# A graph network with mixtures of experts: layer 2's choice of experts moved into the mixture's own stage

## What is computed

```python
h = relu(x @ sW1 + sb1); h = relu(h @ sW2 + sb2); shared = h @ sW3 + sb3     # 256 -> 256 -> 128 -> 256
all_out = the same with 4 experts, 256 -> 128 -> 64 -> 256, for every node
gates = softmax(x @ gW + gb)               # 4 values for each node
topv, topi = top_k(gates, 2)
topw = softmax(topv)                       # of the two chosen gate values
out = shared + sum over the two chosen of topw * all_out[expert]
```

## Time and profile before

| | us |
|---|---|
| median of 3 runs | 3898.34 (3896.64 to 3900.64) |
| the profiled execution, its own time | 3903.26 |
| its span, from the first to the last instruction | 3901.5 |
| TensorE busy | 3152.4 (81%) |
| VectorE busy | 1736.2 (45%) |
| ScalarE busy | 1019.9 (26%) |
| GpSimd busy | 2350.9 (60%) |

### The profile page before, as it was taken

One profiled execution on the slowest core, in us unless ns is written; L12 is line 12 of the kernel. 1 busy time (PEld: TensorE's weight loads), 2 busy tenths in 40 slices (PEclk: granted clock), 3 DMA queues, 4 the chain that ended last, 5 costly groups with the idle time before them and its releaser, 6 DMA issues.

```text
span 3901.5 us, 49195 instructions
## 1 busy us (share of the span) xinstructions
PE 3152.4 (81%) x16263; PEld 2193.2 (56%) x16264; DVE 1736.2 (45%) x4543; ACT 1019.9 (26%) x2155; POOL 2350.9 (60%) x1900
## 2 busy tenths in 40 slices
PE   4999965377787885898079999988998798786798
PEld 3555554256456655788068888875454333334565
DVE  5555545735576775100721112233444444443344
ACT  3666632213546541233221100012120000001121
POOL 6888888888676776677666665540000777772221
PEclk9999996678899995999589999998999655765899
DMA  8663231122557545778444443320213533337232
GB/s 295 183 183 58 5 40 1 1 19 2 163 127 197 135 104 123 209 206 209 80 111 144 137 139 128 133 67 32 95 64 105 150 105 104 103 105 177 74 126 72
DMA packets 284516, 440.11 MB, mean 113 GB/s; under 512 B 167039, under 2 KB 213523, under 8 KB 270565
## 3 DMA queue, kind: packets, MB, share of 16 engines
q1 hardware_dynamic: 118978, 285.09, 23.4%
q0 software_dynamic: 164448, 147.39, 19.4%
q10 hardware_dynamic: 864, 4.80, 0.3%
HBM read 318.97 MB, written 117.63 MB: 112 GB/s over the span
## 4 chain that ended last, share of the span: by engine, by line
PE 38%; POOL 32%; issue 10%; DVE 10%; DMA 7%; DVEq 1%; SPq 1%; ACT 1%; POOLq 0%; ACTq 0%; PEldq 0%
POOL count_cells L484 16%; PE g_acc L2220 14%; POOL g3g_got L1241 9%; PE f2m_pR L2901 4%; POOL weight_cells L1193 4%; PE f3e_pH L3231 3%; PE f2m_pR L2873 3%; PE f3e_pY L3240 3%; DMA f1e_xs<-table,f_node 2%; PE g_acc L1772 2%; DMA g3g_got<-relations,g3g_idx 2%; PE f2m_pO L2884 1%; DMA count_cells<-cells_count,added_row 1%; DMA weight_cells<-added_weight,added_row 1%; PE g_psL L2203 1%
## 5 line engine op out<-in xcount | busy, mean ns | idle before, releaser
L1193 POOL DMA_INDIRECT weight_cells<-added_weight,added_row x391 | 630.5, 1612 | 235.7 <-issue 118.2
L484 POOL DMA_INDIRECT count_cells<-cells_count,added_row x391 | 655.2, 1676 | 141.2 <-issue 118.3
L1241 POOL DMA_INDIRECT g3g_got<-relations,g3g_idx x416 | 398.5, 958 | 545.2 <-ACTq L101 418.8
L2220 PE MATMUL g_acc<-g_H,g_blocks 125*125 125x256 f32 x2500 | 557.3, 382 | 25.6 <-DMA g_blocks<-weight_cells 25.0
L2220 PEld LDWEIGHTS g_acc<-g_H,g_blocks 125*125 125x125 f32 x2500 | 468.6, 189 | 95.6 <-issue 25.4
L2131 POOL DMA_INDIRECT slots_dram<-sort_rec,sort_row x392 | 378.1, 964 | 237.6 <-issue 115.1
L1254 PE MATMUL g3g_pp<-g3g_got,g3g_hot 128*125 128x256 f32 x832 | 436.7, 642 | 104.6 <-DMA g3g_got<-relations,g3g_idx 91.2
L1254 PEld LDWEIGHTS g3g_pp<-g3g_got,g3g_hot 128*125 128x125 f32 x832 | 192.9, 283 | 348.5 <-DMA g3g_got<-relations,g3g_idx 343.4
L1030 ACT ACTIVATE X<-same_scores 128x128 bf16<-128x128 f32 (+7 forms) x392 | 254.7, 650 | 208.4 <-PE same_scores L1019 200.2
L1280 DVE TENSOR_TENSOR X<-X,g3g_pp 125x256 f32 x416 | 175.5, 422 | 290.2 <-PE g3g_pp L1254 248.8
L1844 ACT CAST g_blocks<-g_blocks 128x3125 f16<-128x3125 uint16 x85 | 236.3, 2794 | 29.9 <-DMA g_blocks<-count_cells 29.4
(11 more groups left out here) (728 smaller groups left out, 5598.6 us busy)
## 6 DMA issues: line engine op xcount, KB each, us to landing
g_blocks<-weight_cells SPq DMA_DIRECT2D x50, 1562.5 KB, 6.8
g_blocks<-count_cells SPq DMA_DIRECT2D x85, 781.2 KB, 4.5
weight_cells<-edges_stripe POOLq DMA_DIRECT2D x25, 1562.5 KB
f1e_w<-in_L_ffn_w SPq DMA_DIRECT2D x68, 512.0 KB, 5.2
relations<-f2m_ys SPq DMA_DIRECT2D x25, 896.0 KB
f_w<-in_L_ffn_w SPq DMA_DIRECT2D x16, 1024.0 KB, 7.4
count_cells<-edges_XT POOLq DMA_DIRECT2D x19, 781.2 KB, 31.6
f1e_b<-in_L_ffn_b SPq DMA_DIRECT2D x68, 128.0 KB, 4.6
```

The costliest lines, as they stand in the source:

```text
L484: pool.indirect_dma_start(out=rows, out_offset=bass.IndirectOffsetOnAxis(ap=g.cell_row[:, t:t + 1], axis=0), in_=g.cell_count[:, t:t + 1], ...
L1193: pool.indirect_dma_start(out=rows, out_offset=bass.IndirectOffsetOnAxis(ap=g.cell_row[:, t:t + 1], axis=0), in_=g.cell_weight[:, t:t + 1] ...
L1241: pool.indirect_dma_start(out=got[:, j, :], out_offset=None, in_=table[:, :], in_offset=bass.IndirectOffsetOnAxis(ap=idx[:, n:n + 1], axis ...
L2220: last = nc.tensor.matmul(acc[0:P, i % 3, 0:D], blocks[0:P, i % BLOCKS, t * P:(t + 1) * P], H[p][0:P, t, :], start=(t == 0), stop=(t == T ...
```

## The change

`route` becomes a class `Route`, whose parts are put into streams one by one: `choose` for VectorE, `soften` (the first exponential) and `weigh` (the second) for ScalarE. `route` calls all three in a stage of its own as before, for layer 1. In layer 2 there is no such stage, nor the stage of two instructions behind it. VectorE runs `choose` and the two instructions in the mixture's stage, behind the memset and ahead of the first combination. ScalarE runs `soften` ahead of everything in that stage, and `weigh` in the first mix, ahead of the eviction of piece 4 (the third expert's first layer). The tiles and semaphores of the choice live as long as the mixture's.

```diff
+class Route:
+    def __init__(self, nc, g, ctx, tag, logits, n, first, softmax_first=False, hot=None, weight=None):
...
+        self.centred, self.powers = sem("centred"), sem("powers")
+        self.L = logits[0:P]
+
+    def choose(self, dve):
...
+        if self.softmax_first:
+            nc.vector.tensor_reduce(top[0:P, 0], L, AX, ALU.max)
+            dve.drain()
+            nc.vector.tensor_tensor(L, L, deep(top[0:P, 0], P, T, n), ALU.subtract).then_inc(centred, 1)
+            dve.wait_ge(powers, 1)
+            nc.vector.tensor_reduce(top[0:P, 0], L, AX, ALU.add)
...
+        for k in range(2):
+            nc.vector.tensor_reduce(top[0:P, k], L, AX, ALU.max)
...
+        nc.vector.tensor_tensor(weight[0:P, :, 1], top[0:P, 1], top[0:P, 0], ALU.subtract).then_inc(centred, 1)
+        dve.wait_ge(powers, 2 if self.softmax_first else 1)
+        nc.vector.tensor_scalar(weight[0:P, :, 0], weight[0:P, :, 1], 1.0, None, ALU.add)
...
+    def soften(self, act):
+
+        if self.softmax_first:
+            act.wait_ge(self.centred, 1)
+            self.nc.scalar.activation(self.L, self.L, ACT.Exp).then_inc(self.powers, 1)
+
+    def weigh(self, act):
+
+        second = self.weight[0:P, :, 1]
+        act.wait_ge(self.centred, 2 if self.softmax_first else 1)
+        self.nc.scalar.activation(second, second, ACT.Exp).then_inc(self.powers, 1)
...
-        route(nc, g, "f2r", logits, NE, chosen, softmax_first=True, hot=hot, weight=weight)
-        with stage(nc, g) as block:
-            @block.vector
-            def _(dve):
-
-                nc.vector.tensor_tensor(hot[0:P], hot[0:P], weight[0:P].rearrange("p t (k a) -> p t k a", a=1)
-                                        .broadcast_to([P, T, 2, NE]), ALU.mult)
-                dve.drain()
-                nc.vector.tensor_tensor(coef[0:P], hot[0:P, :, 0, :], hot[0:P, :, 1, :], ALU.add)
+        routing = Route(nc, g, ctx, "f2r", logits, NE, chosen, softmax_first=True, hot=hot, weight=weight)
...
                         rows = H2 if q > 2 + NE else 128
+                        if i == 0 and at == 4:
+                            routing.weigh(act)
                         act.wait_ge(made, i * PIECES + at + 1)
...
+            routing.soften(act)
             for i in range(GROUPS):
                 mix(i)
...
             nc.vector.memset(h2e[H2:H2 + 1, :, :], 1.0).then_inc(set1, 1)
+            routing.choose(dve)
+            dve.drain()
+            nc.vector.tensor_tensor(hot[0:P], hot[0:P], weight[0:P].rearrange("p t (k a) -> p t k a", a=1)
+                                    .broadcast_to([P, T, 2, NE]), ALU.mult)
+            dve.drain()
+            nc.vector.tensor_tensor(coef[0:P], hot[0:P, :, 0, :], hot[0:P, :, 1, :], ALU.add)
             for i in range(GROUPS):
                 combine(i)
```

More of the change, by code:

```diff
@@ L2307, in route @@
 def route(nc, g, tag, logits, n, first, softmax_first=False, hot=None, weight=None):
     with ExitStack() as ctx:
[L2312 to L2316, removed]
+        routing = Route(nc, g, ctx, tag, logits, n, first, softmax_first, hot, weight)
         block = ctx.enter_context(stage(nc, g))
-        iota = wide(g.iota[0:P, 0:n], P, T, n)
@@ L2319, in route @@
-        L = logits[0:P]
         @block.vector
         def _(dve):
-            if softmax_first:
-                nc.vector.tensor_reduce(top[0:P, 0], L, AX, ALU.max)
-                dve.drain()
[L2326 to L2354, removed]
```

28 lines of the change are left out of this document (27 added, 1 removed).

## The result

The changed kernel has a median of 3890.05 us (3884.37 to 3901.83, 20 runs) beside 3898.45 us for the kernel before (3891.64 to 5243.39, 20 runs, one of them far from the rest): a ratio of 0.9978, 95% interval 0.9970 to 0.9985, so 8.4 us less (5.8 to 11.7). Its profiled execution took 3889.88 us.

What follows compares the result with a forecast made beforehand. At the seam TensorE idles 10.97 us behind the expert choice, which its first work does not need. Starting 8.76 us earlier, less 0.18 for the exponential, saves 8.58: 3898.34 - 8.6 = 3889.7 us, range 3885 to 3894.

Steps and rivals of the forecast that it cites:

- steps 1 and 2: Seam before the mixture: TensorE starts 8.76 us earlier without two stages; first exponential costs 0.18 us; 8.58 us saved.
- steps 3 and 4: Mixture: second exponential has 5.9 us of slack, VectorE's moved work 5.8 us of cover before the first combination; no cost.
- steps 5 and 6: Moved SyncE queue issues cost nothing; GpSimd's gathers keep their pace, so the whole chain moves 8.6 us earlier.
- the seventh: TensorE's clock behind the seam: its rise may shift the time 0.45 us either way; taken as 0.
- A: Expected case, whole kernel: the terms hold as summed, 3889.7 us; chance 58%.
- one of the prediction's own signs of being wrong: Mixture: the prediction is wrong if this stage itself grows; no size given.
- step 4: VectorE in the mixture: all 22 moved instructions still run, coefficients ready with 5.8 us of cover; no cost.
- The sum with nothing given back: Seam saving carried whole to the kernel's end: 8.76 less 0.18 is 8.58 us, taken as 8.6.
- C: Rival: ScalarE's table loads hold TensorE's turns or evictions in the mixture, 3891.0 or 3891.8 us; chance 14%.
- D: Rival: saving given back behind the stage, as by a late clock rise (3896.4 us), or never there (3898.3); chance 11%.
- E: Rival: slower, TensorE's clock stays at half through the mixture's first group, up to 3911.1 us; chance 3%.
- B's missed second fall: Rival: TensorE's clock does not fall in the second group, 2.5 us more saved, 3887.2 us; chance 9%.

Runs made afterwards that it cites:

- soften_late: Changed kernel with only the first exponential moved behind the five copies into xT; one run, 3887.7 us.
- free_padded: Changed kernel, TensorE's memset wait moved to the first third-layer product, first exponential behind the copies, second before piece 6, 12 VectorE drains added; ratio to before 0.9966.
- weigh_first: Changed kernel with ScalarE's second exponential right behind the first, ahead of the copies into xT; ratio to the kernel before 0.9996.
- padded: Changed kernel with 12 more drains on VectorE behind the coefficients; ratio to the kernel before 0.9963, timed again 0.9978.
- before_padded: Kernel before, without the change, with 125 more drains on VectorE behind the memset; ratio to the kernel before 1.0009.

## Why the prediction was right, and where it was not

**The seam (steps 1 and 2) was right, term by term.** The memset's gap was taken as 0.65 us and is 0.68; first turn 2.01 us behind the logits, 2.05 measured; seam 5.6, measured 5.53; saved 8.58, measured 8.66. The first exponential's price on the path was taken as 0.18 us; soften_late shows 0.06. Its table load began at 2617.84, ahead of the wait, as argued, and lies under the memset. The Trainium skill ("ScalarE: Activation LUTs", section "What ACT_TABLE_LOAD costs") would have had 2.66 us there; the loads show 1.28 us with the exponential 0.01 to 0.02 us behind it where nothing held it up, last in free_padded, where nothing stands between (2624.22 + 1.28 = 2625.50, 2625.52).

**The second exponential and the coefficients (steps 3 and 4) cost nothing at their own places.** The difference was ready at 2625.36 (2625.18 + 0.18), 5.3 us before ScalarE came (5.9 predicted), no table load stood beside it, and the next eviction began at 2631.42, the usual 0.69 us behind the end of the one before (2630.16 + 0.57 + 0.69 = 2631.42). Cover for the coefficients 6.2 us, 5.8 predicted. weigh_first shows what the place saves.

**GpSimd and layer 3 (steps 5 and 6)** are as said: GpSimd's wait for the indices is 412.5 us where it was 418.8, and the 416 gathers take 960 ns each where they took 958.

**The step that failed is the seventh, "and I take 0" for the clock.** The rise was 0.33 us better (13.79 against 14.12 us for the first 36 products), the fall in the second group stayed (14.48 against 14.60 us) as in A. (The clock's return in that group stands in the prediction as 2689.6; the 0.77 of its row gives 2689.73, 5.05 us behind the dense product and not 4.9, and no term moves by more than 0.1 us.) But a fall that the kernel before does not have was added in the first group, at 3.0 us: one of the prediction's own signs of being wrong, that the mixture's stage itself grows, came true. The cause is in step 4, which priced VectorE's moved work by its duration and its cover alone: it also changed how many instructions stand between the stage's start and the first combination, and so which of them meets the pause. Over all fourteen profiles: where the pause lies in the first tile (8), the clock fell 20.5 to 22.5 us behind the first dense product in 7 and stayed up in soften_late; where it does not (6), it did not fall there. In these seven its first fall is the one that the kernel before has at 2679.5, 38.2 to 40.3 us behind the first dense product. Groups with the added fall take 46.4 to 47.8 us, without it 42.7 to 44.1.

**So the number was met better than its working.** By stretches the changed kernel gains 8.7 at the seam and loses 3.0 to 3.4 in group 1, 5.3 to 5.7 us in all. The timed ratios, 0.9978 (5.8 to 11.7 us) and 0.9982 (3.5 to 10.5 us), give 8.4 and 7.0 us. The first interval's edge just misses the sum, the second holds it. The rest does not lie in what the change touches: from the last logits to layer 3's first gather the changed kernel takes 389.7, 390.8 and 391.4 us in its three profiles, the kernel before 395.5 and 396.5, so 5.4 us less. Behind that gather the two profiles of the first set have 878.8 us before and 880.7 after; ahead of the last logits, in stages that are the same, 2627.1 and 2617.6. So I take the 2 to 3 us over the sum for spread of the other stages, and as not shown to come from the change. By the same stretch padded takes 385.9 and 385.8 us, free_padded 385.5, before_padded 398.5. The sum with nothing given back, 8.6, is reached and passed by padded (57.9 - 48.2 = 9.7 us by stretches, an earlier rise of the clock included).

**The rivals.** C did not come: ScalarE's loads hold nothing. D came in part, by another mechanism than it named: the clock did not rise late, it fell a second time. E did not, and B's missed second fall did not either.

## What to carry to other kernels

When a block of small work stands between two busy stages, look for the one wait of the bounding engine and the one queue that answers it: moving the choice away saves 8.66 us only with the memset ahead of it (else 0.54) and the second exponential not in front of the copies (else 3.6). Then compare the first group behind the seam before and after, since a seam can be won and, as here, a third of it lost 20 us later. An "issue" piece of some tenths of a us on the chain is worth following: if it keeps its place in the instruction stream, a few drains in covered time may move it away, as the 12 did here, while they move every such place behind them too.

## What the runs showed of the hardware that was not expected

VectorE pauses 0.40 us at fixed places of its instruction stream that are 128 instructions apart (134th instruction behind the memset before and in before_padded, there also the 6th; 49th after), and a packet of 8192 bytes of an instruction queue starts 0.66 to 0.96 us behind the pause. In the six profiles without the pause in the first tile the granted clock, once risen, stayed at 1.00 until 38.2 to 40.3 us behind the first dense product (TensorE's wait behind the first tile is 0.59 to 0.61 us); in the eight with it TensorE waited 0.88 or 0.89 us, and in seven of them the clock fell to 0.50, 20.5 to 22.5 us behind the first dense product, for 6.8 us, and group 1 took some 3 us more. A pause of 0.4 us on VectorE can so cost seven times its length on TensorE.
